# Waiting for each scatter and gather to land at the end of an attention and mixture-of-experts kernel

## Chip, cores and metric

The kernel runs on 1 core of one Trainium2 chip. The time is that of one execution on the device, in microseconds (us). Before the change it was 832.31 us, the median of 3 runs (829.86 to 837.1).

## What is computed

32 batches of 256 tokens of width 128, all in float32 at the interface. Each batch goes through a modulated layer norm, attention with 16 heads of width 8, a gated residual, a second modulated layer norm, and a layer of 32 experts of which each token uses the best two. The part that matters here is the last one:

```python
def _L0_ffn_ref(x, router_w, expert_weights):
    TOP_K = 2
    logits = jnp.einsum('bsh,eh->bse', x, router_w)
    rw = jax.nn.softmax(logits, axis=-1).reshape(T, E)
    vals, idx = jax.lax.top_k(rw, TOP_K)
    w_masked = jnp.zeros_like(rw).at[jnp.arange(T)[:, None], idx].set(vals)
    def body(acc, we):
        w_e, W_e = we
        return (acc + x_flat * w_e[:, None] @ W_e, None)
    ...
x = x + ga * _L0_attn_ref(h, ...)
h = _layernorm(x, axis=-1) * (1 + cb) + sb
x = x + gb * _L0_ffn_ref(h, L0_ffn_router_w, L0_ffn_expert_weights)
```

## The kernel before

**Steps.** The work is a software pipeline written out by hand. Every engine runs the same loop over 40 steps; in step s the batches s + 1 down to s - 8 are at successive stages, called `ahead`, `b0` to `b8`. Steps 0 to 34 are attention steps (`attention_step`), steps 35 to 39 are the emptying steps (`drain_step`, from `DRAIN = NB + 3`), and behind them come 12 `turn`s in which TensorE, VectorE and SyncE finish the experts. Nothing reorders instructions: each engine executes its list in the order of the source, and waits on semaphores.

**Experts.** Batches 0 to 29 are treated sparsely. For each batch there are four pairs (two choices, two halves of 128 tokens). GpSimd sends the 128 rows of each pair to the region of their expert in memory by an indirect DMA (`scatter`, L906, from `h2` to `xs_d`; one raises `scat` by 16 when it has landed). When all batches of a chunk (0-7, 8-15, 16-23, 24-29) are there, SyncE loads groups of 4 x 128 rows (`load_group`, L650), TensorE turns them and multiplies them by their expert's weights (L2117, L2132), ScalarE copies the result to `ys_sb` and stores it in `ys_d` (L1151, L1155). There are 62 groups: 0 to 15, 16 to 31, 32 to 47 and 48 to 61. Then GpSimd fetches the results of each pair of a batch by another indirect DMA (`gather`, L921, from `ys_d` to `yg`; 16 on `yg_ld`), and VectorE combines them with the router's weights, the gate and the residual (`combine`, L1620 to L1630), and SyncE stores the batch (L678). Batches 30 and 31 go through all experts densely instead, in 8 quarters (TensorE L2071 and L2087, VectorE L1582).

**Order of the gathers.** Step s names the batches whose gathers it issues: one in each of the steps 25 to 34 (batches 0 to 9), in four places of the attention step between other GpSimd work; batches 10 and 11, 12 and 13, 14 and 15 in steps 35, 36 and 37; 16 and 17 in step 39; 18 to 29 in the loop behind the steps (L976). From step 35 on GpSimd does nothing but the last scatters (one of batch 28, four of batch 29) and these 80 gathers.

**What a gather waits for.** `yg` has `FB = 4` buffers, so the first gather of batch n waits until VectorE has mixed batch n - 4 (`mix_d`, L917). The first gather of a chunk waits besides for the chunk's index (`look`, set by VectorE's L1564) and for the stores of all its groups (`yt_st`). Nothing on GpSimd waits for the landing of a gather; VectorE waits for it (L1616), for all four of a batch:

```python
wait(dve, p_d, b + 1)
wait(dve, yg_ld[i], 64 * (b // FB + 1))
wait(dve, f_ld[i], 32 * (b // FB + 1))
```

**What is queued around them.** SyncE's load of a batch for the combining (L660, L558) waits for the combining of three batches before (L659), and its stores of finished batches (L677) stand in the same queue as the loads of the groups. VectorE's last index table (`look_up(LAST, i)`, L1845) is spread over the turns 0 to 3, ahead of the combining of batch 18 + i. In turn i TensorE does three groups (turns 0 to 2) and one dense quarter (turns 1 to 8).

Of the kernel before, what the change touches and what calls it, by code (L numbers as in the profile page):

```python
# [37 lines left out]
TB = NT // P  # L38
H, HD = 16, 8
E, TOPK = 32, 2  # L40
# [20 lines left out]
FB = 4  # L61
# [25 lines left out]
def chunk_of(n):  # L87

    return next(k for k in CHUNKS if k.lo <= n < k.hi)
# [52 lines left out]
def groups_until(g, i):  # L142

    return (g - i + XB - 1) // XB


def combined_in(s):

    return COMBINED_IN.get(s, [])
# [71 lines left out]
def build(nc, x, Wq, bq, Wk, bk, Wv, bv, Wo, bo, qn_w, kn_w, router_w, expert_w, c_in, wmod, out):  # L221
# [10 lines left out]
    def sem(name):  # L232
        return ctx.enter_context(nc.semaphore(name))
# [4 lines left out]
    with ctx:  # L238
# [203 lines left out]
        scat = [sem(f"scat{i}") for i in range(2)]  # L442
# [7 lines left out]
        yg_ld = [sem(f"yg_ld{i}") for i in range(FB)]  # L450
# [11 lines left out]
        def wait(eng, s, n):  # L462

            if isinstance(n, int) and n <= 0:
                return
            eng.wait_ge(s, n)
# [260 lines left out]
        def _(gp):  # L727
# [170 lines left out]
            @of_sparse  # L898
            def scatter(b, k):

                chunk = chunk_of(b.n)
                if chunk.c >= SETS and b.n == chunk.lo and k == 0:
                    gp.wait_ge(xsT_ps, CHUNKS[chunk.c - SETS].base + CHUNKS[chunk.c - SETS].groups)
                wait(gp, slot_d, b.n + 1)
                gp.nop(nofuse=True)
                nc.gpsimd.indirect_dma_start(xs_d[chunk.set], bass.IndirectOffsetOnAxis(ap=slot[:, b.par, k:k + 1], axis=0),  # L906
                                             h2[:, b.par, k % TB, :], None).then_inc(scat[b.par], 16)

            def gather(n, ks):

                chunk = chunk_of(n)
                if n == chunk.lo and ks[0] == 0:
                    gp.wait_ge(look, 4 * (chunk.c + 1))
                    for i in range(YB):
                        gp.wait_ge(yt_st[i], 16 * groups_until(chunk.base + chunk.groups, i))
                if ks[0] == 0:
                    wait(gp, mix_d, MIX * (n - FB) + 2 * TB)  # L917
                gp.nop(nofuse=True)
                for k in ks:
                    pair = n * TOPK * TB + k  # L920
                    nc.gpsimd.indirect_dma_start(  # L921
                        yg[:, n % FB, k, :], None, ys_d[chunk.c],
                        bass.IndirectOffsetOnAxis(ap=gidx[:, pair:pair + 1], axis=0)).then_inc(yg_ld[n % FB], 16)

            def gather_in(s, *ks):

                for n in combined_in(s):
                    gather(n, ks)
# [29 lines left out]
            def drain_step(s, ahead, b0, b1, b2, b3, b4, b5, b6, b7, b8):  # L958

                if s == DRAIN:  # L960
                    scatter(b7, 3)
                for k in range(TOPK * TB):
                    scatter(b6, k)
                gather_in(s, 0, 1, 2, 3)

            def step(s, *batches):

                if s < DRAIN:
                    attention_step(s, *batches)
                else:  # L970
                    drain_step(s, *batches)
# [2 lines left out]


            for n in range(COMBINED, NS):  # L976
                gather(n, range(TOPK * TB))


        @block.scalar  # L980
# [1291 lines left out]
```

## Time and profile before

| what | value |
|---|---|
| time, median of 3 runs | 832.31 us (829.86 to 837.1) |
| span of the profiled execution, first to last instruction | 977.1 us |
| TensorE busy in it | 751.6 us (77%) |
| VectorE busy | 676.2 us (69%) |
| ScalarE busy | 564.5 us (58%) |
| GpSimd busy | 507.0 us (52%) |
| indirect DMAs on GpSimd | 120 scatters, 120 gathers |
| mean granted TensorE clock | 0.886 |

The profile is one execution, and of its own time the page gives the span; it is 144.8 us longer than the median of the runs. TensorE is PE (its weight loads PEld), VectorE is DVE, ScalarE is ACT, GpSimd is POOL, SyncE is SP; a q behind a name is an engine's DMA queue. Busy time leaves out instructions that only issue plain DMAs or wait; the time of an indirect DMA on GpSimd is what GpSimd spends on issuing it, and its transfer shows only among the DMA packets, on the queue called software_dynamic.

### The profile page before, as it was taken

What the parts mean: (1) busy time and instruction counts of PE and PEld (TensorE: products, weight loads), DVE (VectorE), ACT (ScalarE), POOL (GpSimd) and SP (SyncE); (2) the same over time, 40 slices, a digit from 0 to 9 for tenths busy, and PEclk for the clock granted to TensorE, in tenths of its full rate; (3) what the DMA queues carried; (4) which work ended last, traced back from release to release, by engine and by line L of the source; (5) the groups of instructions that cost most, each with busy time, mean ns of one, the idle gap of its engine ahead of it and who ended that gap; (6) DMA issues with size and microseconds to landing.
All of it is one profiled execution on the core that took longest, in us unless ns stands there. A gap on an engine that the chain in (4) does not pass through costs nothing.

```text
span 977.1 us, 23375 instructions
## 1 busy us (share of the span) xinstructions
PE 751.6 (77%) x6334; PEld 512.0 (52%) x6334; DVE 676.2 (69%) x2015; ACT 564.5 (58%) x1300; POOL 507.0 (52%) x846
## 2 busy tenths in 40 slices
PE   4668988988888889998889788887988762524765
PEld 1234655545554566665666555564655551514665
DVE  4757878878786878788888687788876252611556
ACT  3156877776775778877778676676666522512100
POOL 5112455566654555555556666676665535273253
PEclk8579999999997999999999999999898765766888
DMA  2555545466444567767566666665554433754632
GB/s 66 146 146 142 117 115 148 120 150 151 123 115 122 152 168 183 179 175 181 158 179 177 178 161 172 162 167 152 152 154 122 128 108 86 211 154 133 183 81 81
DMA packets 178001, 141.70 MB, mean 145 GB/s; under 512 B 19540, under 2 KB 162612, under 8 KB 177876
## 3 DMA queue, kind: packets, MB, share of 16 engines
q1 hardware_dynamic: 122804, 99.54, 39.8%
q10 hardware_dynamic: 47392, 24.92, 8.8%
q0 software_dynamic: 7680, 15.74, 5.8%
q8 instruction: 57, 0.93, 0.5%
q14 instruction: 68, 0.56, 0.2%
HBM read 81.77 MB, written 57.80 MB: 143 GB/s over the span
## 4 chain that ended last, share of the span: by engine, by line
PE 39%; DVE 15%; issue 14%; DMA 9%; another core or an unknown queue 9%; SPq 7%; ACT 5%; POOL 1%; ACTq 0%; DVEq 0%; POOLq 0%
PE mx_ps L1937 10%; PE st_ps L1972 7%; PE o_ps L1986 6%; DVE negmax L1397 5%; DMA k_aug<-k_d 4%; DMA k_d<-parts 4%; PE st_ps L2132 3%; SPq L650 2%; PE misc L1995 2%; PE misc L1910 2%; SPq L602 2%; ACT pr L1089 2%; PE st_ps L2117 1%; PE misc L2029 1%
## 5 line engine op out<-in xcount | busy, mean ns | idle before, releaser
L1397 DVE TENSOR_REDUCE negmax<-mx_ps 128x2 f32<-128x512 f32 x512 | 339.0, 686 | 123.4 <-PE mx_ps L1937 68.1
L1089 ACT ACTIVATE pr<-st_ps 128x512 f32<-128x512 f32 x512 | 285.2, 599 | 77.9 <-PE st_ps L1972 71.9
L1937 PE MATMUL mx_ps<-k_aug,q_aug 126*128 126x256 bf16 x1024 | 200.1, 287 | 68.0 <-DVE negmax L1397 26.0
L1972 PE MATMUL st_ps<-q_aug,k_aug 128*128 128x256 bf16 x1024 | 190.5, 285 | 0.8 <-ACT ys_sb L1151 0.3
L1986 PE MATMUL o_ps<-pr,v_aug 128*32 128x256 f32 x2048 | 145.7, 404 | 37.4 <-issue 31.4
L921 POOL DMA_INDIRECT yg<-ys_d,gidx x120 | 117.7, 981 | 95.6 <-DVE yb L1627 42.0
L1937 PEld LDWEIGHTS mx_ps<-k_aug,q_aug 126*128 126x128 bf16 x1024 | 84.3, 100 | 158.3 <-issue 148.2
L906 POOL DMA_INDIRECT xs_d<-h,slot x120 | 120.5, 1004 | 59.2 <-DVE slot L1500 33.9
L1972 PEld LDWEIGHTS st_ps<-q_aug,k_aug 128*128 128x128 bf16 x1024 | 101.4, 105 | 30.1 <-issue 11.1
L1986 PEld LDWEIGHTS o_ps<-pr,v_aug 128*32 128x32 f32 x2048 | 57.3, 112 | 89.2 <-issue 69.5
L1095 ACT ACTIVATE oT<-o_ps 128x256 f32<-128x256 f32 x128 | 49.2, 384 | 77.7 <-remote 43.3
L781 POOL TENSOR_TENSOR qn<-qkvg,rstd 128x256 f32<-128x256 f32 x64 | 39.1, 635 | 83.3 <-DVE rstd L1313 83.3
L2117 PE MATMUL st_ps<-ident,xs_sb 128*128 128x128 f32 x248 | 41.9, 299 | 34.8 <-DMA xs_sb<-xs_d 22.0
L794 POOL TENSOR_TENSOR parts<-rest,parts 128x512 bf16<-128x512 f32 x32 | 37.1, 1158 | 52.5 <-ACT parts L1077 52.5
L1910 PE MATMUL misc<-wq_b,hT 128*128 128x400 f32 x128 | 58.5, 545 | 1.0 <-ACT hT L1028 0.9
L1151 ACT ACTIVATE ys_sb<-mx_ps 128x512 f32<-128x512 f32 x25 | 14.9, 596 | 65.7 <-remote 42.6
L2117 PEld LDWEIGHTS st_ps<-ident,xs_sb 128*128 128x128 f32 x248 | 32.2, 156 | 37.8 <-issue 37.1
L1995 PE MATMUL misc<-ident,oT 128*128 128x128 f32 x256 | 43.3, 297 | 10.9 <-ACT oT L1095 7.4
L1146 ACT ACTIVATE xsT<-st_ps 128x512 f32<-128x512 f32 x62 | 36.5, 596 | 24.2 <-PE st_ps L2117 20.1
L2132 PE MATMUL mx_ps<-we,xsT 128*128 x200 | 37.2, 347 | 13.8 <-ACT xsT L1146 9.9
L2132 PE MATMUL st_ps<-we,xsT 128*128 x296 | 42.6, 288 | 2.8 <-issue 1.4
L1366 DVE TENSOR_TENSOR qkvg<-misc,bias_p 128x400 f32<-128x400 f32 x64 | 36.0, 564 | 12.0 <-PE misc L1910 6.7
(192 smaller groups left out, 1280.3 us busy)
## 6 DMA issues: line engine op xcount, KB each, us to landing
xs_sb<-xs_d SPq DMA_DIRECT2D x248, 64.0 KB
ys_d<-ys_sb ACTq DMA_DIRECT2D x62, 256.0 KB
q_aug<-q_d SPq DMA_DIRECT2D x64, 192.0 KB
mod_o<-mod_d SPq DMA_DIRECT2D x32, 256.0 KB
bias_p<-bias_d SPq DMA_DIRECT2D x32, 200.0 KB
q_d<-parts SPq DMA_DIRECT2D x32, 192.0 KB, 2.1
k_d<-parts SPq DMA_DIRECT2D x32, 192.0 KB, 2.5
k_aug<-k_d SPq DMA_DIRECT2D x64, 96.0 KB
```

Source lines behind the costliest of these rows:

```text
L906: nc.gpsimd.indirect_dma_start(xs_d[chunk.set], bass.IndirectOffsetOnAxis(ap=slot[:, b.par, k:k + 1], axis=0), h2[:, b.par, k % TB, :], No ...
L921: nc.gpsimd.indirect_dma_start(yg[:, n % FB, k, :], None, ys_d[chunk.c], bass.IndirectOffsetOnAxis(ap=gidx[:, pair:pair + 1], axis=0)).the ...
L1089: nc.scalar.activation(pr[:, h % PR], st_ps[score_bank(b, h)][:], ACT.Exp, scale=SCALE).then_inc(exp_d, 1)
L1095: nc.scalar.activation(oT[:, g, :], o_ps[:, 0:NT], ACT.Copy).then_inc(oT_d, 1)
L1397: v.tensor_reduce(negmax[:, :, h], mx_ps[h % 2][:], AX.X, ALU.max, negate=True).then_inc(mx_d, 1)
L1910: t_.matmul(bank[:, 0:QKVG], hT[:, t * P:(t + 1) * P], wq_b[:, b.par], start=True, stop=True).then_inc(qkv_ps, 1)
L1937: last = t_.matmul(mx_ps[h % 2][:, qc], q_aug[b.par][0:MROW, h, qc * P:(qc + 1) * P], k_aug[b.par][0:MROW, h, :], start=True, stop=True)
L1972: last = t_.matmul(st_ps[score_bank(b, h)][:, kc], k_aug[b.par][:, h, kc * P:(kc + 1) * P], q_aug[b.par][:, h, :], start=True, stop=True)
L1986: last = t_.matmul(o_ps[32 * j:32 * j + VW, 0:NT], v_aug[b.par][:, kc, h, :], pr[:, h % PR, kc, :], start=(kc == 0), stop=(kc == TB - 1))
L1995: last = t_.transpose(bank[:, g * P:(g + 1) * P], oT[:, g, qc * P:(qc + 1) * P], ident[:])
L2117: last = t_.transpose(in_bank(g)[:, k * P:(k + 1) * P], xs_sb[:, g % XB, k, :], ident[:])
L2132: last = t_.matmul(out_bank(g)[:, k * P:(k + 1) * P], xsT[g % XB][:, k * P:(k + 1) * P], we[:, bass.ds(columns[k], P)], start=True, stop=True)
```

## The change

In the emptying steps GpSimd waits, behind each of the four scatters of batch 29, until that scatter has landed (its semaphore stands at 16 more). Gathers are issued one at a time, in the same order as before, and behind each GpSimd waits until that gather has landed. The loop behind the steps does the same. The attention steps are unchanged. `of_sparse` calls a function only for the batches 0 to 29; `b.nth` is half the batch's number, `b.par` its parity.

```diff
--- before.py
+++ after.py
@@ -906,6 +906,10 @@
                 nc.gpsimd.indirect_dma_start(xs_d[chunk.set], bass.IndirectOffsetOnAxis(ap=slot[:, b.par, k:k + 1], axis=0),
                                              h2[:, b.par, k % TB, :], None).then_inc(scat[b.par], 16)
 
+            @of_sparse
+            def scatter_landed(b, k):
+                gp.wait_ge(scat[b.par], 64 * b.nth + 16 * (k + 1))
+
             def gather(n, ks):
 
                 chunk = chunk_of(n)
@@ -961,7 +965,11 @@
                     scatter(b7, 3)
                 for k in range(TOPK * TB):
                     scatter(b6, k)
-                gather_in(s, 0, 1, 2, 3)
+                    scatter_landed(b6, k)
+                for n in combined_in(s):
+                    for k in range(TOPK * TB):
+                        gather(n, [k])
+                        gp.wait_ge(yg_ld[n % FB], 64 * (n // FB) + 16 * (k + 1))
 
             def step(s, *batches):
 
@@ -974,7 +982,9 @@
 
 
             for n in range(COMBINED, NS):
-                gather(n, range(TOPK * TB))
+                for k in range(TOPK * TB):
+                    gather(n, [k])
+                    gp.wait_ge(yg_ld[n % FB], 64 * (n // FB) + 16 * (k + 1))
 
 
         @block.scalar
```

GpSimd's list at the first emptying step, before the change, with the semaphores that each instruction waits for (L906 is a scatter, L921 a gather):

```order
699 L906 DMA xs_d<-h,slot 69632x128 [waits slot_d] x5
700 L921 DMA yg<-ys_d,gidx 128x128 [waits mix_d]
701 L921 DMA yg<-ys_d,gidx 128x128 x3
702 L921 DMA yg<-ys_d,gidx 128x128 [waits mix_d]
703 L921 DMA yg<-ys_d,gidx 128x128 x3
```

The same place in the changed kernel, where the gather's line is L925:

```order
699 L906 DMA xs_d<-h,slot 69632x128 [waits slot_d] x2
700 L906 DMA xs_d<-h,slot 69632x128 [waits scat1,slot_d] x3
701 L925 DMA yg<-ys_d,gidx 128x128 [waits scat1,mix_d]
702 L925 DMA yg<-ys_d,gidx 128x128 [waits yg_ld2] x3
703 L925 DMA yg<-ys_d,gidx 128x128 [waits yg_ld2,mix_d]
704 L925 DMA yg<-ys_d,gidx 128x128 [waits yg_ld3] x3
```

The instructions and their order are the same; each but the first two scatters now waits for the one before it. The last batch of the loop behind the steps, before:

```order
738 L921 DMA yg<-ys_d,gidx 128x128 [waits mix_d]
739 L921 DMA yg<-ys_d,gidx 128x128 x3
740 L238 UNCONDITIONAL_BRANCH
```

and in the changed kernel:

```order
739 L925 DMA yg<-ys_d,gidx 128x128 [waits yg_ld0,mix_d]
740 L925 DMA yg<-ys_d,gidx 128x128 [waits yg_ld1] x3
741 L238 UNCONDITIONAL_BRANCH [waits yg_ld1]
```

Here too only the waits are new, the last one behind the last gather. The lists of the other engines have the same instructions in the same order.

## Rows read from the trace of the kernel before

**Rows 1.** The page: the chain by engine, two groups, queues, DMA issues.

```profile
PE 39%; DVE 15%; issue 14%; DMA 9%; another core or an unknown queue 9%; SPq 7%; ACT 5%; POOL 1%; ACTq 0%; DVEq 0%; POOLq 0%
...
L921 POOL DMA_INDIRECT yg<-ys_d,gidx x120 | 117.7, 981 | 95.6 <-DVE yb L1627 42.0
...
L906 POOL DMA_INDIRECT xs_d<-h,slot x120 | 120.5, 1004 | 59.2 <-DVE slot L1500 33.9
...
q0 software_dynamic: 7680, 15.74, 5.8%
...
q_d<-parts SPq DMA_DIRECT2D x32, 192.0 KB, 2.1
k_d<-parts SPq DMA_DIRECT2D x32, 192.0 KB, 2.5
```

**Rows 2.** Busy time of each engine by stretch (last columns: clock, DMA share, GB/s).

```profile
60.00:285.00 225.00, 197.10 (x1766) 121.29 (x1765) 181.57 (x520) 163.34 (x385) 113.87 (x210) 0.94 0.52 132
500.00:760.00 260.00, 217.65 (x1966) 147.89 (x1962) 197.04 (x592) 175.88 (x410) 163.42 (x276) 0.94 0.62 162
795.00:977.00 182.00, 96.00 (x622) 85.45 (x621) 77.46 (x237) 34.67 (x63) 81.64 (x84) 0.74 0.46 134
806.00:821.00 15.00, 0.29 (x3) 0.06 (x1) 0.00 (x0) 1.11 (x2) 11.41 (x12) 0.61 0.28 76
865.00:885.00 20.00, 1.09 (x4) 0.72 (x4) 3.66 (x10) 0.39 (x1) 15.42 (x16) 0.50 0.31 83
930.00:937.00 7.00, 2.62 (x21) 2.19 (x20) 0.84 (x3) 0.00 (x0) 4.14 (x5) 0.90 0.35 94
```

The columns are, in this order: stretch, us, TensorE, its weight loads, VectorE, ScalarE, GpSimd.

**Rows 3.** GpSimd's instructions in order of time: start us, us, instruction, idle before.

```profile
774.95 1.01 POOL L921 DMA_INDIRECT yg<-ys_d,gidx  x1
...
795.46 0.97 POOL L906 DMA_INDIRECT xs_d<-h,slot  x1 [12.24 <-DVE slot L1500]
...
828.56 0.99 POOL L921 DMA_INDIRECT yg<-ys_d,gidx  x1 [7.77 <-DVE yb L1627]
...
854.85 0.95 POOL L921 DMA_INDIRECT yg<-ys_d,gidx  x1 [15.97 <-DMA ys_d<-ys_sb]
856.11 0.95 POOL L921 DMA_INDIRECT yg<-ys_d,gidx  x1 [0.30 <-issue]
...
899.38 0.99 POOL L921 DMA_INDIRECT yg<-ys_d,gidx  x1 [14.39 <-DVE yb L1627]
...
925.49 0.95 POOL L921 DMA_INDIRECT yg<-ys_d,gidx  x1 [5.76 <-DVE gidx L1564]
...
953.63 0.99 POOL L921 DMA_INDIRECT yg<-ys_d,gidx  x1 [2.58 <-DVE yb L1627]
...
962.46 0.95 POOL L921 DMA_INDIRECT yg<-ys_d,gidx  x1 [0.30 <-issue]
```

**Rows 4.** Waits from 790 us on: total us, times, longest.

```profile
ACT ys_sb L1151 <- remote: 42.6, 5, 19.8
POOL yg L921 <- DVE yb L1627: 42.0, 7, 14.4
...
DVE table L1545 <- remote: 21.6, 1, 21.6
```

**Rows 5.** DMA packets from 964.1 to 964.7 us: packets, MB, share.

```profile
q0 software_dynamic: 32, 0.07, 42.5%
```

**Rows 6.** DMA packets from 964.7 to 977 us, all of one queue.

```profile
DMA packets 864, 0.79 MB, mean 64 GB/s; under 512 B 96, under 2 KB 864, under 8 KB 864
## 3 DMA queue, kind: packets, MB, share of 16 engines
q1 hardware_dynamic: 864, 0.79, 18.5%
```

**Rows 7.** DMA packets from 776.6 to 778.2 us, by queue.

```profile
q1 hardware_dynamic: 136, 0.06, 28.5%
q10 hardware_dynamic: 258, 0.13, 26.7%
q0 software_dynamic: 32, 0.07, 16.2%
```

**Rows 8.** VectorE in order of time near the end.

```profile
952.27 0.61 DVE L1624 SCALAR_TENSOR_TENSOR yc<-yg,p_all,yw 128x128 f32<-128x128 f32 x2
...
971.98 0.47 DVE L1620 TENSOR_SCALAR yw<-yg,p_all 128x128 f32<-128x128 f32 x2
...
973.47 0.42 DVE L1630 TENSOR_TENSOR of<-yb,x_f 128x256 f32<-128x256 f32 x1
```

**Rows 9.** DMA packets from 770 us to the end.

```profile
DMA packets 40342, 27.22 MB, mean 131 GB/s; under 512 B 4464, under 2 KB 38773, under 8 KB 40325
...
q0 software_dynamic: 2848, 5.84, 10.5%
```

## Prediction

> **What bounds the kernel now.** I read the page first, then tables by stretch, then GpSimd's rows in order of time, then the DMA packets. The chain that ended last is 39% TensorE and 15% VectorE [rows 1], and the indirect DMAs are 240 short GpSimd instructions of about 1 us: the bound differs by stage, and the change sits in one stage only. That stage begins at the four scatters of batch 29, the first of which starts at 795.46 us [rows 3], and fills the last 181.6 us of 977.1.
>
> The table by stretch [rows 2] shows three kinds of time. In the attention steps (60 to 285, 500 to 760) VectorE is busy 81% and 76%. From 795 to 977 no engine is: TensorE 96.0 of 182 us, VectorE 77.5, GpSimd 81.6. Inside it lie stretches in which only GpSimd works: from 806 to 821 TensorE has 3 matmuls and VectorE nothing while GpSimd starts 12 gathers, and from 865 to 885 TensorE has 4 matmuls against 16 gathers. The largest wait of ScalarE there, 42.6 us, and a single one of VectorE, 21.6 us, have the releaser "remote" [rows 4], that is, none that the profile can name. So in this trace a long unbroken row of gathers goes together with a stop of everything else.
>
> GpSimd itself is not the bound in this stage. Its rows in order of time [rows 3] show bursts: one indirect DMA each 1.26 us (0.95 busy, 0.30 "issue"), with pauses: 7.77 us until VectorE freed a buffer, 15.97 us until the last expert rows of a chunk were stored, 14.39 us until VectorE again. Its waits for VectorE's combining are 42.0 us [rows 4]. Those pauses are the slack that the change uses up.
>
> **The change, part by part.** No instruction is added that computes or moves data. Four scatters and 80 gathers get a wait for their own landing behind them: 84 landings. The scatter of batch 28 that goes ahead of them keeps none. All 84 stand in one row on GpSimd with nothing else between them, so the cost is (cycle now minus cycle before) times the row, less the pauses.
>
> *One landing.* The packets tell it. A scatter or gather makes 7680/240 = 32 packets on the software queue [rows 1]. The last gather starts at 962.46 [rows 3]; all its 32 packets lie in 964.1 to 964.7 and none after 964.7 [rows 5, 6]: 2.2 us from start to landing, on quiet queues. The gather that starts at 774.95 [rows 3] has its 32 packets inside 776.6 to 778.2, amid 394 packets of the hardware queues [rows 7]: 3.25 us. Plain DMAs of 192 KB take 2.1 and 2.5 us to land [rows 1].
>
> *From the landing to the next start.* The wait stands on the next DMA. The nearest rows are GpSimd's waits for VectorE: its instruction ends at 952.27 + 0.61 = 952.88, and the released gather starts at 953.63 [rows 8, 3]: 0.75 us. A burst has only the 0.30 of issue. I take 0.75.
>
> *The cycle.* From below 2.2 + 0.75 = 2.95 us, from above 3.25 + 0.75 = 4.0 us. I take 3.2, nearer the quiet end: the stage moves 27.22 MB from 770 on, of which 5.84 is the software queue's own [rows 9]; the other 21.4 MB over some 270 us are 79 GB/s, while the stage before had 134 [rows 2].
>
> *The sum, in the profiled execution.* From the first scatter to the last gather's start are 83 cycles: 83 x 3.2 = 265.6 us, where before they took 962.46 - 795.46 = 167.0. Behind the last start come 2.2 us of landing and the combining of the last batch up to the end of the span, 977.1 - 971.98 = 5.1 us [rows 8], and some 0.3 to wake VectorE: 7.6. In all 795.5 + 265.6 + 7.6 = 1068.7 us against 977.1: 91.6 us more.
>
> *Does anything else wait longer than that?* Gather n waits until VectorE has combined n - 4. At 4 x 3.2 = 12.8 us per batch that is always long past, as combining costs VectorE 1.9 us a batch [rows 8]. The first gather of chunk 2 (batch 16) waits for the stored rows of group 47, which before were there at 854.85; GpSimd now reaches it at 795.5 + 28 x 3.2 = 885. That of batch 24 waits for the last chunk's index and rows, before at 925.49; GpSimd now reaches it at 795.5 + 60 x 3.2 = 987.5. SyncE's loads of the last groups are queued behind its loads and stores of batches 16 and 17, VectorE's table of the last chunk behind the combining of batch 20: both stand at least three batches (38 us) ahead. The dense quarters of TensorE and VectorE fall in GpSimd's waits and cost nothing. So every pause of [rows 3] is covered, and the stage becomes GpSimd's row alone. Where a stop goes because gathers no longer run back to back, nothing is gained: what was stopped is no longer what the end waits for.
>
> *A rule on the landing.* The row shows 2.2 us quiet and 3.25 us in traffic [rows 5 to 7]. The Trainium skill, page "DMA: Bandwidth & Descriptors", section "Anatomy of one DMA — SWDGE (gpsimd) path", puts one such DMA at about 2.0 us fixed plus bytes over 436e3, mostly the receipt of the last write, whatever else moves. For 64 KB that is an estimate of 2.15 us, and the sum by it would be 795.5 + 83 x 2.9 + 7.6 = 1044 us. The quiet row agrees with it, the row in traffic does not.
>
> **From the profiled execution to the median.** The page gives the span, 977.1 us; the median of the runs is 832.31, so 144.8 us of the profiled execution are not in a plain one. Where they lie decides what the sum is worth there.
> - Reading one: the stops of [rows 2] belong to the profiled execution: 15 + 20 + 7 = 42 us. The rest scales by 832.3/935.1 = 0.89: the part ahead of the scatters is 708 us, the cycle 0.89 x 3.2 = 2.85 us, and the changed kernel takes 708 + 83 x 2.85 + 6.8 = 951 us. An unscaled cycle would give 981.
> - Reading two: everything scales by 0.852: 1068.7 x 0.852 = 910 us.
> - Reading three: the excess is a constant: 832.3 + 91.6 = 924 us.
>
> I take reading one, as a stop with an unnamed releaser, of all engines at once, is what an instrumented execution would add, and so large a surplus has to lie somewhere: 951 us, 14% more.
>
> **The rivals.**
> - *Short landings or an even scale* (readings two and three, or a cycle at its lower bound): 0.852 x (795.5 + 83 x 2.95 + 7.6) = 893 us to 924. For it: the quiet row of 2.2 us, and a plain execution may land faster still. Against: the surplus isn't even, since stops stand in three places. 0.25.
> - *Landings in traffic throughout*: a cycle of 4.0: 708 + 83 x 0.89 x 4.0 + 7 = 1011 us. For it: the software queue shares its engines with SyncE's and ScalarE's transfers. Against: these are spread thinner. 0.12.
> - *The other side: bursts hold the other engines, and spaced gathers give them their time back.* Place: the stops at 806 to 821, 865 to 885, 930 to 937; price: up to 42 us gained in the profiled execution. It decides only if GpSimd's own row fits beneath the old end: 708 + 83 x cycle + 7 below 832 needs a cycle under 1.41 us, and a landing alone is 2.2. Then some 830 us. 0.02.
> - *The change doesn't do what it says*: a threshold already reached, a wait that passes at once, 832 us. The counts (64 per four batches of a buffer, 16 for each landing) fit exactly. 0.01.
>
> **How the numbers follow.** Forecast 0.60: 951 us. Low end 893 (cycle 2.95, even scale), rounded to 890; high end 1011, rounded to 1010. A measurement of this kernel tells about 1% from no change. Every case but the last two is slower by 7% or more: slower 0.97, the same 0.02, faster 0.01.
>
> **What would show it.** In the changed profile: GpSimd's gathers start 2.9 to 4.0 us apart from the first scatter to the end, their idle time before them is put down to DMA or to waits of 2 us each, and the pauses for VectorE and for the stored rows are gone; the stretches in which the others had 0 to 4 instructions are gone too; the span is 1030 to 1100 us; the time ahead of the scatters is unchanged. Wrong would be: starts at 1.3 us (the wait does nothing), starts under 2 us (my landing is an artefact), or a pause of more than 10 us left on GpSimd (another engine bounds the stage). If the profiled span grows by 90 us and the median by much less or more, the mapping failed and not the sum.

## The result and the profile after

The changed kernel takes 1006.95 us, the median of 4 runs (1006.29 to 1016.59), beside 834.7 us for the kernel before in the same comparison: a ratio of 1.209, interval 1.201 to 1.216. The forecast was 951 us, within 890 to 1010.

GpSimd's rows in order of time answer to [rows 3]. Columns: start us, us, instruction, idle before and what ended it.

```profile
710.47 0.96 POOL L906 DMA_INDIRECT xs_d<-h,slot  x1 [7.76 <-DVE slot L1510]
714.68 0.97 POOL L906 DMA_INDIRECT xs_d<-h,slot  x1 [3.25 <-DMA xs_d<-h,slot]
...
725.10 0.98 POOL L925 DMA_INDIRECT yg<-ys_d,gidx  x1 [2.25 <-DMA xs_d<-h,slot]
729.56 0.96 POOL L925 DMA_INDIRECT yg<-ys_d,gidx  x1 [3.48 <-DMA yg<-ys_d,gidx]
732.84 0.95 POOL L925 DMA_INDIRECT yg<-ys_d,gidx  x1 [2.32 <-DMA yg<-ys_d,gidx]
...
995.94 0.95 POOL L925 DMA_INDIRECT yg<-ys_d,gidx  x1 [2.21 <-DMA yg<-ys_d,gidx]
```

The bursts and pauses of before are one even row: 84 starts, of which the last comes 285.5 us after the first, so 83 cycles of 3.44 us in the mean, and each idle time is ended by a landing. The row starts at 710.5, where [rows 3] has 795.5; that is the surprise of this case, and the experiments take it up.

The group of these gathers, from 725 to 997 us (busy us, mean ns, idle before by releaser):

```profile
L925 POOL DMA_INDIRECT yg<-ys_d,gidx x80 | 76.2, 953 | 197.8 <-DMA yg<-ys_d,gidx 145.7 <-DVE yw L1630 42.3 <-issue 7.6
```

197.8/80 = 2.47 us of idle time and 0.95 of issue make the cycle. The 42.3 us put down to VectorE are most likely landings too: they stand at the first gather of 17 batches, where VectorE's combining (L1630) has just been released by the landing that GpSimd waits for, and they are as long as the others (42.3/17 = 2.49 us). The longest waits from 705 us on, and the chain of the page, answer to [rows 4] and [rows 1]:

```profile
DVE yw L1630 <- DMA yg<-ys_d,gidx: 149.4, 16, 16.1
POOL yg L925 <- DMA yg<-ys_d,gidx: 145.7, 60, 3.7
...
PE misc L2081 <- DVE q_aug L1592: 57.8, 7, 20.7
```

```profile
DMA 20%; issue 8%; DVE 2%; PE 0%; POOLq 0%; DVEq 0%; ACT 0%; POOL 0%; ACTq 0%
DMA yg<-ys_d,gidx 19%; DMA xs_d<-h,slot 1%; DVE yw L1630 1%; PE mx_ps L2142 0%; DVE dsl L1572 0%; PE misc L2005 0%; DVE yc L1634 0%; POOLq L922 0%; DVE yb L1637 0%; DVEq L466 0%; DVE ydw L1602 0%; DVE topi L1461 0%; DVE v_aug L1605 0%; ACT oT L1105 0%; DVE fac L1423 0%
```

VectorE waits for gathers in 16 of the 20 batches, TensorE's dense quarters wait for VectorE, and the chain that ended last, which the page follows back over some 30% of the span, is nearly all landings of gathers and the issuing of the next. The stage by stretch, answering to [rows 2]:

```profile
710.00:820.00 110.00, 36.32 (x207) 32.67 (x206) 27.38 (x111) 25.01 (x47) 30.65 (x32) 0.66 0.40 113
820.00:930.00 110.00, 50.18 (x313) 45.52 (x313) 33.81 (x79) 9.34 (x16) 29.47 (x31) 0.73 0.29 83
930.00:1005.00 75.00, 17.15 (x106) 16.06 (x105) 17.12 (x47) 0.00 (x0) 19.97 (x21) 0.62 0.13 38
```

TensorE is busy a third of the time, VectorE a quarter. No wait in this profile is put down to "remote".

### The profile page after: what moved, and what is told of

Same layout as the page of the kernel before. It is cut to its first block and busy times, and to the rows that moved or that the text cites. A ratio compares the mean times of both kernels' runs of the same rounds, so it can differ in the third digit from the quotient of the medians.

```text
span 1005.8 us, 23438 instructions
## 1 busy us (share of the span) xinstructions
PE 725.1 (72%) x6334; PEld 503.1 (50%) x6334; DVE 676.4 (67%) x2015; ACT 565.2 (56%) x1300; POOL 504.6 (50%) x846
## 5 line engine op out<-in xcount | busy, mean ns | idle before, releaser
L1099 ACT ACTIVATE pr<-st_ps 128x512 f32<-128x512 f32 x512 | 285.5, 598 | 55.6 <-PE st_ps L1982 54.3
L1947 PE MATMUL mx_ps<-k_aug,q_aug 126*128 126x256 bf16 x1024 | 189.7, 279 | 57.0 <-DMA k_aug<-k_d 33.4
L925 POOL DMA_INDIRECT yg<-ys_d,gidx x120 | 116.3, 969 | 207.6 <-DMA yg<-ys_d,gidx 145.7
L1982 PE MATMUL st_ps<-q_aug,k_aug 128*128 128x256 bf16 x1024 | 181.3, 275 | 0.3 <-DMA q_aug<-mrows 0.3
L906 POOL DMA_INDIRECT xs_d<-h,slot x120 | 120.4, 1004 | 62.0 <-DVE slot L1510 29.0
L1630 DVE TENSOR_SCALAR yw<-yg,p_all 128x128 f32<-128x128 f32 x60 | 14.4, 280 | 190.0 <-DMA yg<-ys_d,gidx 149.4
L1996 PE MATMUL o_ps<-pr,v_aug 128*32 128x256 f32 x2048 | 137.3, 385 | 4.1 <-ACT oT L1105 3.7
L1982 PEld LDWEIGHTS st_ps<-q_aug,k_aug 128*128 128x128 bf16 x1024 | 97.4, 100 | 24.6 <-issue 8.4
L1996 PEld LDWEIGHTS o_ps<-pr,v_aug 128*32 128x32 f32 x2048 | 54.9, 109 | 52.8 <-issue 31.7
L2081 PE MATMUL misc<-wdT,k_aug 96*128 96x256 bf16 x64 | 15.8, 340 | 57.9 <-DVE q_aug L1592 57.8
L2142 PEld LDWEIGHTS mx_ps<-we,xsT 128*128 128x128 f32 x200 | 32.7, 248 | 48.1 <-issue 47.9
```

What stands on the lines that cost most here:

```text
L925: nc.gpsimd.indirect_dma_start(yg[:, n % FB, k, :], None, ys_d[chunk.c], bass.IndirectOffsetOnAxis(ap=gidx[:, pair:pair + 1], axis=0)).the ...
L1099: nc.scalar.activation(pr[:, h % PR], st_ps[score_bank(b, h)][:], ACT.Exp, scale=SCALE).then_inc(exp_d, 1)
L1947: last = t_.matmul(mx_ps[h % 2][:, qc], q_aug[b.par][0:MROW, h, qc * P:(qc + 1) * P], k_aug[b.par][0:MROW, h, :], start=True, stop=True)
L1982: last = t_.matmul(st_ps[score_bank(b, h)][:, kc], k_aug[b.par][:, h, kc * P:(kc + 1) * P], q_aug[b.par][:, h, :], start=True, stop=True)
L1996: last = t_.matmul(o_ps[32 * j:32 * j + VW, 0:NT], v_aug[b.par][:, kc, h, :], pr[:, h % PR, kc, :], start=(kc == 0), stop=(kc == TB - 1))
L2142: last = t_.matmul(out_bank(g)[:, k * P:(k + 1) * P], xsT[g % XB][:, k * P:(k + 1) * P], we[:, bass.ds(columns[k], P)], start=True, stop=True)
```

## The experiments

Each comparison put its kernels and the kernel before on one chip together. The kernel before took about 835 us in some comparisons and 968 to 977 us in others; below they are called the 835 and the 970 setting. The record names the chip: 9 in the first two comparisons below and 14 in the last were in the 970 setting, 5 was in the 835 setting; for the comparison of the result none is named. So the setting may belong to the chip, but no run tries that. What makes one or the other wasn't found, so each kernel is compared with the kernel before of its own comparison.

**The kernel before, profiled again.** No edit.

> The kernel before, unchanged, profiled again. My theory: the 144.8 us by which its first profiled execution exceeded the median were the profiled execution's own (stops of all engines beside rows of gathers, and a slower part ahead), so a second one may differ much; the time without a profile is 834.7 us as before. In an undisturbed profile the last batch's first scatter starts near 710 us, as in the changed kernel (710.47), and GpSimd's row from there to the last gather is close to its floor of 83 x 1.26 = 105 us, with 5 to 20 us of pauses. Rival: the stops belong to rows of back-to-back gathers and stand in this profile too, at the same three places, with the span again near 977 us.

Measured: 968.98 us beside 968.57, in plain runs; span 969.2. So the long span of the profile before was not the profiled execution's own: unprofiled runs take as long. In this profile the last scatters start at 793.9 us. Its waits, over the whole kernel:

```profile
ACT ys_sb L1151 <- remote: 45.1, 8, 13.4
ACT oT L1095 <- remote: 42.2, 21, 6.3
```

and two stretches of it, the columns as in [rows 2]:

```profile
802.00:818.00 16.00, 0.41 (x4) 0.17 (x2) 0.00 (x0) 2.08 (x4) 12.34 (x13) 0.60 0.34 94
860.00:878.00 18.00, 1.09 (x4) 0.71 (x4) 4.62 (x13) 0.60 (x1) 13.74 (x15) 0.50 0.37 103
```

The same stops at the same places. The rival was right and my theory wrong: the "remote" waits and the stops are found in plain conditions too, and they go with the 970 setting, as no profile taken in the 835 setting has any.

**One part of the change alone.** Three kernels, each the kernel before with one hunk of the change:

```diff
 # e1: scatters
                     scatter(b6, k)
+                    scatter_landed(b6, k)
 # e2: the loop behind the steps
+                    gather(n, [k])
+                    gp.wait_ge(yg_ld[n % FB], 64 * (n // FB) + 16 * (k + 1))
 # e3: the same two lines for combined_in(s) in drain_step
```

> Only the four scatters of the last sparse batch are waited for. Theory (the stage is GpSimd's row, 3.44 us per waited DMA instead of 1.26): at most 4 x 2.2 = 9 us more, less the pauses of the kernel before: 835 to 844 us. Rival (the pauses of before are long and absorb the first waits): no change, 835 us.

> Only the 48 gathers of the loop behind the steps are waited for. Theory: from the first of them on the row takes 48 x 3.44 = 165 us; it is reached at 710 + 36 x 1.26 = 755 us plus pauses of up to 15 us, and 10 us follow the last start: 930 to 945 us. Rival (the waits of the emptying steps do the harm, because SyncE's and VectorE's queues for later work stand behind the first combinings): under 900 us.

> Only the 32 gathers of the emptying steps are waited for. Theory: 710 + 4 x 1.26 + 32 x 3.44 = 825 us to the first gather of the loop, then 48 x 1.26 = 60 us and 10 us: 895 us, up to 905 if a pause is left in the loop. Rival (queues for later work stand behind the first combinings): over 920 us. If all is one row, the excess over before of the three parts adds up to that of the whole, 172 us, plus the pauses of before once or twice.

Measured, all beside 968.57: scatters 971.08 (1.003, 0.999 to 1.007), loop 1033.45 (1.068), emptying steps 1009.76 (1.044). The scatters' excess can't be told from none. The expectations assumed the 835 setting. Carried over for the loop, with the start of its first gather as the repeated profile of before has it (859.7 us), the row gives 859.7 + 47 x 3.44 + 10 = 1031 us, and the profile's span is 1030.7. The loop's first gathers and the last in that profile:

```profile
856.79 0.95 POOL L921 DMA_INDIRECT yg<-ys_d,gidx  x1 [0.30 <-issue]
860.07 1.09 POOL L921 DMA_INDIRECT yg<-ys_d,gidx  x1 [2.33 <-issue]
...
1020.79 0.95 POOL L921 DMA_INDIRECT yg<-ys_d,gidx  x1 [2.27 <-DMA yg<-ys_d,gidx]
```

47 cycles in 164.0 us, 3.49 each. The third kernel is a miss: carried over, its theory gives 794 + 5 + 32 x 3.44 + 60 + 10 = 979 us. The first gather of the loop starts at 914.51, where that sum has 909, but then come bursts again, 48 gathers from 914.51 to 993.25 us, 1.68 apart instead of 1.26. They hold a pause of 10.4 us for the last chunk's index table, and in that stretch VectorE has a long wait with an unnamed releaser, of the kind that went with rows of gathers before:

```profile
DVE q_aug L1585 <- remote: 25.2, 3, 18.5
POOL yg L921 <- DVE gidx L1567: 10.4, 1, 10.4
```

The excesses are 2.5, 64.9 and 41.2 us, 108.6 together, beside 116.9 for the whole change (next run): the parts add up to within 8 us, which the interval of the whole (about 10 us to either side) doesn't tell from nothing. The rival for these, that waits early would do more harm than their own row by holding up later queues, isn't seen in the excess: 32 gathers cost 1.29 us each, 48 cost 1.35. But the time of the third kernel lies where the rival, carried over, would have it (920 + 84 = 1004 or more), and the late index table could be such a queue. The trace speaks for the stop instead: VectorE's 18.5 us end at 949.00, the table stands behind them in its list, and the waiting gather starts at 955.98. No run here separates the two.

**The change in the 970 setting.** No edit.

> The changed kernel again, beside runs of the kernel before on the same chip. In the first comparison before took 834.7 us; in the second 968.6, with the last batch's first scatter at 794 instead of 710 us and waits of the other engines put down to remote. Theory (GpSimd's row of 83 cycles of 3.44 us is the whole stage, on either chip): if before takes 835 here, this one takes 1007 again; if before takes 968, this one takes 794 + 83 x 3.42 + 11 = 1089 us, a ratio of 1.12. Rival (spaced gathers take the stops away and the kernel reaches the same end on either chip): 1007 us on both.

Measured: 1089.18 us beside 972.3, ratio 1.124 (1.114 to 1.134). The forecast was 1089. In the profile the row begins at 791.2 us, and its gathers are as in the first profile of the changed kernel:

```profile
L925 POOL DMA_INDIRECT yg<-ys_d,gidx x80 | 76.2, 953 | 197.7 <-DMA yg<-ys_d,gidx 145.9 <-DVE yw L1630 42.0 <-issue 7.7
```

The row is the same in both settings to 0.1 us; only what stands ahead of it differs, by 81 us. The stops in the emptying steps are gone, and nothing is gained by that, as the end waits for the row.

**Waits for two at a time.**

```diff
+                    for k in range(0, TOPK * TB, 2):
+                        gather(n, [k, k + 1])
+                        gp.wait_ge(yg_ld[n % FB], 64 * (n // FB) + 16 * (k + 2))
```

> Gathers go out two at a time, and only then GpSimd waits for both; scatters as before. Theory (each wait costs the landing of one gather, 2.2 us, and 1.06 us to the next start, once per two gathers): a pair takes 1.26 + 3.4 = 4.65 us, 40 pairs 186 us, with 5 us for the scatters and 10 us behind: 710 + 201 = 911 us where before takes 835; 794 + 201 = 995 where before takes 968. Rival (cost per gather waited for, or the landing grows with two in flight): near the changed kernel, over 960 or 1040.

Measured: 1005.84 us beside 972.3 (1.039). From its profile:

```profile
934.31 0.95 POOL L921 DMA_INDIRECT yg<-ys_d,gidx  x1 [3.67 <-DMA yg<-ys_d,gidx]
935.56 0.95 POOL L921 DMA_INDIRECT yg<-ys_d,gidx  x1 [0.30 <-issue]
938.91 0.95 POOL L921 DMA_INDIRECT yg<-ys_d,gidx  x1 [2.40 <-DMA yg<-ys_d,gidx]
```

The pair takes 4.6 us when the landing is quick, as 934.31 to 938.91, and 1.3 more when it isn't, as the idle time of 3.67 us before it shows. The mean is 5.06 us: 40 x 0.41 = 16 us over the forecast, less 6 because the first scatter starts at 788.2 instead of 794, and 11 were measured. The cost goes by waits, not by gathers.

**Two in flight.** `yg_ld` has two semaphores per buffer, by the parity of k; VectorE waits for both.

```diff
+                    j = TOPK * TB * n + k - 2
+                        gp.wait_ge(yg_ld[m % FB][i % 2], 32 * (m // FB) + 16 * (i // 2 + 1))
                     gather(n, [k])
```

> Each gather waits for the landing of the one before the last, so that two are in flight (two semaphores per buffer, one per parity of the gather). Theory: a gather starts at the earliest 3.3 us after the one before the last, 1.65 us apart on average: 80 x 1.65 + 15 = 147 us: 710 + 147 = 857, or 794 + 147 = 941 plus the pauses of before, so no change there (968). Rival (the cost is in waiting as such, not in the depth): like the pairs or worse.

> The kernel with two gathers in flight again, in five rounds: it was 1.4% faster than before (0.975 to 0.997) where before took 972 us. Theory: the same ratio where before takes 970, as the stops of 794 to 820 and 850 to 875 us are broken up; where before takes 835 there are no stops, and it is 857 us, 2 to 3% slower. Rival (the gain was chance): 1.00 on either chip.

Measured: 958.97 us beside 972.3 in the 970 setting (0.986, 0.975 to 0.997, a gain of under 2%), and 879.48 beside 835.12 in the other (1.053, 1.050 to 1.055). The sign turns with the setting, as the second expectation has it; the first had 968 and no change. The size in the 835 setting was forecast at 857. The row shows why: 79 cycles from 715.2 to 870.8 us are 1.97 each, not 1.65, and in the 970 setting they are 1.96. From one gather to the next but one it is 3.3 us at the quickest quarter and 4.3 or more at the slowest quarter, in both settings. So with two in flight more landings are slow; why, no run shows.

**A wait that has long been met.** Behind each gather `gp.wait_ge(gp_const, IOTAS + 6)`.

> Behind each of the 80 gathers stands a wait that has long been met, for a constant's semaphore. Theory (the landing costs, not the wait instruction): no change, within 1% of before. Rival (a wait in front of an indirect DMA keeps GpSimd from preparing it, so that each costs 0.7 us whether met or not): 80 x 0.7 = 56 us more, less the pauses, 880 or 1000 us.

Measured: 971.2 us beside 972.3 (0.999, 0.994 to 1.004). The wait as an instruction costs nothing that can be measured. The time between a wait's end and the next start (0.75 us behind VectorE in [rows 3, 8]) is paid only when the wait was still open.

**No gathers at all.** `nc.gpsimd.memset(yg[:, n % FB, k, :], 0.0)` instead of the indirect DMA, so the rows of the sparse experts are left out of the result.

> All 120 gathers are replaced by memsets of their buffers (the rows of the experts are not fetched, the output lacks them); scatters and everything else as before. It shows what lies beneath GpSimd's row, and whether the stops of the other engines come with the indirect DMAs. Theory (where before takes 968 us, each indirect DMA holds up all engines for a while): the stops in the emptying steps are gone, the steps 25 to 34 are shorter by some 3 us each, and the end comes 100 us behind the last scatters, which start at 755 to 765: 860 us. Where before takes 835: 710 + 100 = 810. Rival (the stops have another cause, the slower part ahead lies in the chip): the steps 25 to 34 keep their 25 us and the waits put down to remote stay.

Measured, in the 835 setting: 832.48 us beside 835.12 (0.997, 0.994 to 0.999). Its busy times behind the attention steps:

```profile
710.00:829.00 119.00, 83.30 (x604) 75.63 (x602) 74.84 (x225) 33.23 (x60) 13.77 (x82) 0.87 0.53 155
```

My 810 was wrong, and so was the picture behind it that GpSimd's row alone sets the end of before. Without a gather the other engines need 832. GpSimd's own floor is an estimate, 83 x 1.26 from 710 and 8.5 behind it: 823. So in the 835 setting the kernel before lies 3 us above what the others need and some 12 us above GpSimd's floor. Whether the stops come with the gathers this run could not show, as no profile taken in this setting has any.

**Gathers spaced by other work.** Behind each gather a memset of `spare`, 128x256 or 128x512; no landing is waited for.

```diff
+                    gather(n, [k])
+                    wait(gp, spaced_d, done)
+                    nc.gpsimd.memset(spare[:], 0.0).then_inc(spaced_d, 1)
```

> Behind each of the 80 last gathers GpSimd does a memset of 128x256, some 0.3 to 0.4 us; nothing waits for a landing. Theory (a gather that does not start at once behind the one before leaves the other engines their turn): starts 1.6 us apart, the same as with two in flight: 958 us where before takes 970, 835 to 857 where before takes 835. Rival (two in flight was faster because of the queue's depth, not of the pace): 970 to 985 us where before takes 970.

> The memset behind each of the 80 last gathers is 128x512 instead of 128x256, some 0.6 us instead of 0.33, so that gathers start 1.72 us apart instead of 1.45; no landing is waited for. Theory where before takes 835 us: the stage is GpSimd's row from 1.4 us a gather on, so 708 + 5 + 79 x 1.72 + 8.4 = 857 us, 2.7% slower (the shorter memset gave 845, 1.3% slower). Theory where before takes 970: the same row behind 789 us gives 939 us, 3% faster than before, if gathers that start 1.72 us apart stop nobody; with the other engines as the bound some 950. Rival there (what helped with two in flight was that each landing is awaited, not the pace): 970 us or more.

The short one, in the 835 setting: 844.98 us beside 835.12 (1.013, 1.009 to 1.017), within the 835 to 857 expected. The long one, in the 970 setting: 940.46 beside 977.31, ratio 0.963 (0.959 to 0.968), the forecast 939. Its row, and two stretches where the kernel before stood still:

```profile
803.42 0.99 POOL L924 DMA_INDIRECT yg<-ys_d,gidx  x1 [0.30 <-issue]
804.41 0.54 POOL L933 MEMSET spare<- 128x512 f32 x1
805.12 0.97 POOL L924 DMA_INDIRECT yg<-ys_d,gidx  x1 [0.17 <-issue]
...
936.48 0.96 POOL L924 DMA_INDIRECT yg<-ys_d,gidx  x1 [0.17 <-issue]
```

```profile
800.00:815.00 15.00, 6.37 (x40) 5.33 (x39) 6.58 (x32) 4.73 (x10) 13.05 (x17) 0.73 0.52 148
855.00:875.00 20.00, 13.18 (x69) 11.20 (x70) 6.13 (x15) 6.66 (x12) 18.05 (x24) 0.76 0.76 211
```

40 matmuls in 15 us where the repeated profile of before has 4 in 16. GpSimd does 80 memsets more than before and the kernel is 37 us faster: in this setting it is the unbroken row of indirect DMAs that holds the other engines. Waits with an unnamed releaser, from the last scatters on and over all engines, say the same: 70.2 us in the repeated profile of before, 13.5 with the long memset, 11.1 with two in flight, 3.1 with pairs, none in the changed kernel. The gain needs no wait for a landing, as there is none here. Beside two in flight the starts are closer, 1.68 us apart instead of 1.96, and the time is 940 against 959 us, though on another chip.

All of it goes by one number. With c the mean distance of the gathers' starts, the span of a profile is the start of the first scatter, plus the four scatters, 79 c, and what follows the last start:

```
setting   kernel            first   scatters   c      79 c    behind   span     median time
835       spaced, short     708.2    5.1       1.48   117.1   8.5      838.8     844.98
835       two in flight     710.1    5.1       1.97   155.6   8.1      878.9     879.48
835       changed kernel    710.5   14.6       3.43   270.8   9.9     1005.8    1006.95
970       spaced, long      798.3    5.1       1.68   133.1   8.7      945.2     940.46
970       two in flight     789.4    5.1       1.96   155.0   8.3      957.8     958.97
970       pairs             788.2    5.1       2.53   199.8   9.9     1003.0    1005.84
970       changed kernel    791.2   14.6       3.43   270.8   9.9     1086.6    1089.18
```

The parts add up to the span by the way they are taken. What the table shows is that within a setting the first column moves by some 10 us and the last part by 2, so c sets the end (with the 10 us of the scatters' waits in the changed kernel). Two times were forecast in this way before the runs, 1089 and 939 us, and came out as 1089.18 and 940.46; where the forecast missed, with pairs and with two in flight, c was the term. Below c = (832 - 708 - 5 - 8.5)/79 = 1.4 us in the 835 setting the other engines should take over at 832, an estimate.

## Why the prediction was right, and where it wasn't

The measured time lies inside the range, and the mechanism, one row of GpSimd with a landing in each cycle, was right. That it lies inside is in part luck: it is 56 us above the forecast and 3 below the upper end, which came from a rival that fell.

- **The stage becomes GpSimd's row alone**: right. Every pause of [rows 3] is gone, the chain is gathers, and the parts of the change add up as parts of one row do.
- **No rest of a pause**: right. The longest idle time in the row is 3.97 us, and 53 of 79 gaps from gather to gather are under 3.3 us.
- **One landing, 2.2 to 3.25 us**: right for most. The gather that starts at 729.56 has its 32 packets in 731.1 to 731.8, 2.2 us behind its start; the slowest cycle of the row, 4.92 us up to 870.84, leaves 3.9 us for its landing.

```profile
q0 software_dynamic: 32, 0.07, 30.8%
```

- **From the landing to the next start, 0.75 us**: the term that was mis-sized. That gather's last packet lies before 731.8 and the next starts at 732.84, 1.05 us later. The rows used, GpSimd's waits for VectorE [rows 3, 8], show the time behind an engine's end; behind the last packet of a DMA it is 0.3 us more, and what fills these 0.3 no row shows. The quick cycle is so 2.2 + 1.05 = 3.25 us, and half of the gaps are 3.26 or less; slower landings bring the mean to 3.44, where 3.2 allowed 0.25 for them. 83 cycles are 285.5 us, not 265.6. In the 970 setting, to which the profile before belongs by its span, the sum of 1068.7 us became a span of 1086.6, 18 us more: 20 of the row, 2 behind it, and 4 less ahead of it.
- **Behind the last start, 7.6 us**: 9.9 measured (1005.8 - 995.94).
- **From the profiled execution to the median**: the step that failed. Reading one said that the stops, and a slower part ahead, belonged to the profiled execution. They belong to the setting, which plain runs show too (968.98 us). Its value for the time ahead of the scatters, 708 us, came out (710.5), but by luck: the comparison was made in the 835 setting, which is faster by about that factor ahead of the scatters (710.5/795.5 = 0.89), for a reason that is not the profiler. Its second half, to shrink the cycle by 0.89 along with everything else, failed: a gather's cycle is 3.43 us in both settings. Put right, the sum is 710.5 + 285.5 + 9.9 = 1005.9 us, and the miss of 55 us below that span is 49 of the row (83 x 3.44 for 83 x 2.85), 2.5 ahead of it and 3 behind. The unscaled value that stood beside the forecast, 981, was nearer. Two of the named signs failed with this step: the profiled span was 1005.8 us, not 1030 to 1100, and the time ahead of the scatters was not that of the profile before.
- **The even scale and the constant excess** (893 to 924): fell. So did "landings in traffic throughout" as a mechanism, although its 1011 us is nearest: half of the cycles are 3.26 us or less, which leaves the quiet 2.2 us for the landing.
- **The other side, spaced gathers give the others their time back**: false for this change, true as a mechanism in the 970 setting. There it brings 3.7% at 1.68 us a gather; at 3.43 us the row has long overtaken it, as the condition of this rival said.
- **A rule on the landing**: the fixed cost that the Trainium skill gives ("DMA: Bandwidth & Descriptors", section "Anatomy of one DMA — SWDGE (gpsimd) path"), an estimate of 2.15 us for one gather, fits the quick landings of 2.2 us and not the slow ones. The sum by it, 1044 us, lies 43 below the 1086.6 of the 970 setting: it lacks the same 0.3 us per wait, 25 us, and the slow landings, some 16.

## What to carry to other kernels

A wait for each landing behind a short DMA costs the landing and the time to the next start, here a cycle of 3.43 us instead of 1.26, and it is paid once per wait: multiply the cycle by the length of the row and add it to the row's start, not to the old end. Whether an engine's row sets the end must be measured by leaving its work out (832 of 835 us remained here), not read from its pauses. Before a profile's surplus over the median is put down to profiling, run the same kernel again: the surplus may be a condition that plain runs share, and a change can have another size, or another sign, in it.

## What the hardware showed that was not expected

- Two settings of one kernel, 835 and 970 us, steady within a comparison. Up to the first scatter they agree (it starts between 129.0 and 130.8 us in the 835 setting and between 127.3 and 131.2 in the other), and they part in the very next step. The first scatters of the first two batches, in the changed kernel's profile (835) and in the repeated one of before (970):

```profile
129.04 1.19 POOL L906 DMA_INDIRECT xs_d<-h,slot  x1 [1.19 <-DVE slot L1510]
...
147.53 1.02 POOL L906 DMA_INDIRECT xs_d<-h,slot  x1 [1.35 <-issue]
```

```profile
130.29 1.19 POOL L906 DMA_INDIRECT xs_d<-h,slot  x1 [1.19 <-DVE slot L1500]
...
152.42 1.03 POOL L906 DMA_INDIRECT xs_d<-h,slot  x1 [1.35 <-issue]
```

  That is 18.5 us for the step against 22.1. The last batch's first scatter starts at 710.5 and 793.9.

- In the 970 setting a row of indirect DMAs 1.26 us apart leaves the other engines almost no instruction (4 matmuls in 16 us); at 1.68 us apart they run (40 in 15 us). In the 835 setting the short spacing only costs, 1.3%. What is shared, and why only in one setting, stays open; that the slower attention steps of the 970 setting, 22.9 us from scatter to scatter instead of 20.0, have the same cause is possible but wasn't tried.
- GpSimd starts an indirect DMA 1.05 us after the last packet of the one that it waited for, but 0.30 us behind its own instruction before when nothing is waited for, and 80 waits that had been met cost nothing (0.999 of the time, 0.994 to 1.004).
